# The experts' first loads, statistics and products, moved across the border from attention

## Chip, cores and metric

The kernel runs on one core of one Trainium2 chip. The metric is the device time of one execution in microseconds (us), as the median of several runs. Traces are of one profiled execution.

## What is computed

Input x has 64 batches of 64 rows of 256 numbers. Four residual steps, each on a layer-normalized x: cross attention, a mixture of eight experts beside a shared one (this is where the change lies), a gated pooling attention, a second feed-forward network.

```python
def _L0_ffn_ref(hidden_states, gate_w, w_gate_up, w_down, shared_gate_up, shared_down):
    x = hidden_states.reshape(-1, 256)
    shared_out = _silu_and_mul(x @ shared_gate_up) @ shared_down
    probs = softmax(x @ gate_w, axis=-1)
    topk_w, topk_i = lax.top_k(probs, 2)
    topk_w = topk_w / jnp.sum(topk_w, axis=-1, keepdims=True)
    combine = jnp.sum(one_hot(topk_i, 8) * topk_w[..., None], axis=1)
    ...
    return moe_out + shared_out

x = x + tanh(g_xattn[0]) * _L0_xattn_ref(_layernorm(x), ctx_2048, ...)
x = x + tanh(g_ffn[0]) * _L0_ffn_ref(_layernorm(x), ...)
x = x + tanh(g_xattn[1]) * _L1_xattn_ref(_layernorm(x), ctx_2048, ...)
x = x + tanh(g_ffn[1]) * _L1_ffn_ref(_layernorm(x), ...)
```

## The kernel before

All 4096 rows of x stay in on-chip memory as 32 tiles of 128 rows. Three functions run one after the other, each a block of its own with one instruction stream per engine: `attention`, `experts`, `gate_and_ffn`. The streams meet at semaphores alone, and each engine takes its instructions in the order in which they are written, so that order sets the order of the work. Engines are TensorE (PE), VectorE (DVE), ScalarE (ACT), GpSimd (POOL) and SyncE (SP, which here issues transfers).

**Attention** is a pipeline over tiles. `steps` calls `body(n, n, 0)` for some first n, a hardware loop for the middle and then n = 26 to 33. In `body(n)` an engine works on several tiles at once: scores of tile n+1, exponentials and products of tile n, the output of tile n-2. In the last bodies (n = 31, 32, 33) only the late parts are left; this is the drain. DVE's `normalize_out` (L413, L417), PE's turns and the output product (L592, L631, L652), ACT's copies (L480, L484, L488) and POOL's addition into x (L341) form its chain. SP's last instruction is `q_st<-m_rows` of tile 31 (L241), for which PE waits before the score products of tile 31 (`m_stacked`, in `score_step`).

**Experts**, first half: for eight groups of 512 rows (four tiles) the router and the shared expert. For a group j:

- DVE `stats_of(j)`, POOL `rstd_of(j)` (1/sqrt by a power of -0.5, L929 and L932), DVE `shift_of(j)`, ACT `norm_of(j)` (L1048) make normalized rows `xn`.
- PE `turn(j)` (L1482) transposes them into `t_ps`, ACT `high_of(j)` (L1040) and DVE `low_of(j)` (L1155) split the result into a high and a low part: products are made of three matmuls, high by high, low by high, high by low.
- PE `make_wide(j)` (L1491) multiplies by the router's weights, ACT `take_wide(j)` (L1061) copies, PE `make_logits(j)` (L1499) folds, DVE `take_logits(j)` (L1172) reads the logits. DVE `choose(j)` picks two experts a row, ACT `lead_of(j)` (L1055) takes a tanh for the shares, PE `rank(j)` (L1510) counts rows, DVE `slots_of(j)` (from L1225) gives the places, and POOL `send(j)` scatters the rows to memory.
- PE `products(g, m)` (L1522, twelve matmuls, m = 0 to 3, two banks of each result in turn), ACT's silu (L1089), DVE's product (L1406), ACT `high` and DVE `low` (L1398), PE `down(g, m)` (L1534) are the shared expert. PE may fill a bank for m only when the silu and the product of m-2 are done.

Its weights come in three pieces of 512 KB (`stage`, two buffers); `first_high(p)` (ACT, L1066) and `first_low(p)` (DVE, L1162) split them. The second half runs the eight experts over sorted tiles.

PE's order at the start, before:

```python
turn(0)
pe.wait_ge(s["router_split"], 1)
make_wide(0)
make_logits(0)
turn(1)
make_wide(1)
...
for g in range(GROUPS):
    if g == 0:
        pe.wait_ge(s["first_split"], 2)
    for m in range(CHUNKS):
        products(g, m)
```

## Time and profile before

| what | value |
|---|---|
| median of 3 runs | 1432.47 us (1432.46 to 1432.76) |
| the profiled execution | 1434.49 us, span 1432.8 us |
| PE, DVE, ACT, POOL busy | 93%, 65%, 53%, 48% of the span |
| mean granted clock of PE | 0.969 of full speed |

From the page, in 40 slices of 35.8 us each (tenths of busy time; PEclk: tenths of the full clock):

```profile
PE   4899999999999589998998999999987999999998
DVE  7799999999997278766554333333335766665553
ACT  0477777777778544432342333333426656665642
POOL 7577777777772156443675223310044554445210
PEclk9999999999999789999999999999976999999999
```

The fourteenth slice, from 466 to 501 us, is the border between attention and the experts. A "busy" engine is executing, an idle one waits at a semaphore or has nothing; timelines give behind each instruction the idle time ahead of it and what ended it. The span is from the first to the last instruction, and the profiled execution's own time is 1.7 us more than its span.

### The profile page before, as it was taken

What the parts mean: (1) busy time and instruction counts of PE and PEld (TensorE: products, weight loads), DVE (VectorE), ACT (ScalarE), POOL (GpSimd) and SP (SyncE); (2) the same over time, 40 slices, a digit from 0 to 9 for tenths busy, and PEclk for the clock granted to TensorE, in tenths of its full rate; (3) what the DMA queues carried; (4) which work ended last, traced back from release to release, by engine and by line L of the source; (5) the groups of instructions that cost most, each with busy time, mean ns of one, the idle gap of its engine ahead of it and who ended that gap; (6) DMA issues with size and microseconds to landing.
All of it is one profiled execution on the core that took longest, in us unless ns stands there. A gap on an engine that the chain in (4) does not pass through costs nothing. (4 is left out here: it accounts for less than half of the span.)

```text
span 1432.8 us, 31669 instructions
## 1 busy us (share of the span) xinstructions
PE 1334.9 (93%) x9954; PEld 1017.8 (71%) x9955; DVE 925.9 (65%) x1689; ACT 756.2 (53%) x1461; POOL 686.2 (48%) x853
## 2 busy tenths in 40 slices
PE   4899999999999589998998999999987999999998
PEld 3555555555555268887877888888876788888887
DVE  7799999999997278766554333333335766665553
ACT  0477777777778544432342333333426656665642
POOL 7577777777772156443675223310044554445210
PEclk9999999999999789999999999999976999999999
DMA  3222222222221122114732333241131110111000
GB/s 103 79 81 83 79 88 82 73 86 85 78 73 38 51 83 80 60 59 138 238 124 82 97 97 95 67 142 51 45 96 41 30 44 28 34 45 30 15 16 30
DMA packets 85891, 105.53 MB, mean 74 GB/s; under 512 B 11249, under 2 KB 76145, under 8 KB 85425
## 3 DMA queue, kind: packets, MB, share of 16 engines
q1 hardware_dynamic: 75344, 70.38, 15.5%
q0 software_dynamic: 10464, 34.09, 7.5%
q8 instruction: 47, 0.77, 0.2%
q14 instruction: 36, 0.29, 0.1%
HBM read 53.05 MB, written 23.99 MB: 54 GB/s over the span
## 5 line engine op out<-in xcount | busy, mean ns | idle before, releaser
L469 ACT ACTIVATE e_t<-st_ps 128x512 f32<-128x512 f32 x512 | 278.5, 597 | 105.5 <-PE st_ps L557 101.9
L407 DVE TENSOR_REDUCE row_max<-s_ps 128x4 f32<-128x1024 f32 x256 | 311.3, 1218 | 21.8 <-PE s_ps L562 19.5
L584 PE MATMUL o_ps<-e_t,v_st 128*32 128x256 f32 x2048 | 166.5, 398 | 0.1
L557 PE MATMUL st_ps<-q_st,k_st 32*128 32x256 f32 x1024 | 160.5, 333 | 6.2 <-DMA q_st<-m_rows 3.6
L562 PE MATMUL s_ps<-k_st,q_st 32*128 32x256 f32 x1024 | 158.1, 342 | 5.1 <-DVE row_max L407 3.5
L557 PEld LDWEIGHTS st_ps<-q_st,k_st 32*128 32x128 f32 x1024 | 106.1, 187 | 56.0 <-issue 36.3
L1773 POOL DMA_INDIRECT gathered_tail<-sorted_results,result_at x64 | 70.8, 1106 | 125.3 <-POOLq L2299 107.2
L1640 PE MATMUL y_ps_moe<-w_all_moe,xt_hi_moe 128*128 x568 | 116.5, 286 | 7.7 <-DVE xt_lo_moe L1440 7.7
L2039 DVE TENSOR_TENSOR h_all_tail<-silu_tail,u_ps_tail 128x512 f32<-128x512 f32 x64 | 43.8, 685 | 118.7 <-ACT silu_tail L1888 64.5
L1446 DVE TENSOR_TENSOR h_all_moe<-silu_moe,u_ps_moe 128x512 f32<-128x512 f32 x71 | 48.8, 687 | 109.3 <-PE u_ps_moe L1609 109.3
L1124 ACT COPY y_sb_moe<-y_ps_moe 128x256 f32<-128x256 f32 x71 | 26.5, 373 | 162.2 <-PE y_ps_moe L1640 162.2
L562 PEld LDWEIGHTS s_ps<-k_st,q_st 32*128 32x128 f32 x1024 | 104.3, 193 | 7.1 <-DVE row_max L407 4.6
L1609 PE MATMUL g_ps_moe<-w_all_moe,xt_hi_moe 128*128 x284 | 107.3, 418 | 0.0
L1640 PEld LDWEIGHTS y_ps_moe<-w_all_moe,xt_hi_moe 128*128 128x128 f32 x568 | 93.4, 190 | 12.3 <-issue 9.5
L1609 PE MATMUL u_ps_moe<-w_all_moe,xt_hi_moe 128*128 x284 | 101.0, 396 | 0.0
L952 POOL DMA_INDIRECT sorted_rows<-xn_moe,slots_moe x64 | 64.6, 1009 | 51.8 <-DVE slots_moe L1235 34.5
L1436 DVE TENSOR_TENSOR xt_lo_moe<-t_ps_moe,xt_hi_moe 128x256 fp32r<-128x256 f32 x71 | 30.1, 424 | 91.2 <-ACT xt_hi_moe L1106 91.2
L1888 ACT ACTIVATE silu_tail<-g_ps_tail 128x512 f32<-128x512 f32 x64 | 38.0, 594 | 85.3 <-PE g_ps_tail L2209 85.1
L1640 PE MATMUL y_ps_moe<-w_all_moe,xt_lo_moe 128*128 x284 | 80.7, 284 | 0.0
L2221 PE MATMUL y_ps_tail<-w_hi,h_hi_tail 128*128 128x256 f32 x256 | 74.5, 291 | 0.5 <-DVE h_lo_tail L2046 0.5
L1114 ACT ACTIVATE silu_moe<-g_ps_moe 128x512 f32<-128x512 f32 x71 | 42.5, 599 | 58.9 <-PE g_ps_moe L1609 58.9
L2221 PE MATMUL y_ps_tail<-w_lo,h_hi_tail 128*128 128x256 f32 x256 | 72.8, 284 | 0.0
(341 smaller groups left out, 3613.7 us busy)
## 6 DMA issues: line engine op xcount, KB each, us to landing
k_st<-k_part SPq DMA_DIRECT2D x96, 128.0 KB, 2.1
q_st<-q_part SPq DMA_DIRECT2D x96, 128.0 KB
stage_moe<-in_experts POOLq DMA_DIRECT2D x21, 512.0 KB, 4.2
rows_in_moe<-sorted_rows SPq DMA_DIRECT2D x71, 128.0 KB, 2.0
sorted_results<-y_sb_moe SPq DMA_DIRECT2D x71, 128.0 KB, 1.7
c_in<-in_ctx SPq DMA_DIRECT2D x32, 128.0 KB, 2.2
x_sb<-in_x SPq DMA_DIRECT2D x32, 128.0 KB, 2.1
xn_moe<-in_ctx SPq DMA_DIRECT2D x8, 512.0 KB, 4.4
```

The lines of the kernel that those rows point to most:

```text
L407: nc.vector.tensor_reduce(out, s_ps[p % 2][:], AX_X, ALU.max).then_inc(s["max_taken"], 1)
L469: nc.scalar.activation(e_t[t % 4][:, b, :, :], st_ps[:, b, :, :], ACT.Exp, scale=float(DH) ** -0.5)\
L557: last = nc.tensor.matmul(out, w, moving, start=True, stop=True)
L562: last = nc.tensor.matmul(out, w, moving, start=True, stop=True)
L584: last = nc.tensor.matmul(o_ps[32 * j:32 * j + 32, :], values[:, at:at + 32], e_t[(2 * u + j // 2) % 4][:, j % 2, half_, :], start=(half_ ...
L952: pool.indirect_dma_start(out=xs[:, :], out_offset=bass.IndirectOffsetOnAxis(ap=slots[:, w, GT * j + t:GT * j + t + 1], axis=0), in_=xn[j ...
L1446: nc.vector.tensor_tensor(h_all[c % 2][:], silu[c % 2][:], u_ps[c % 2][:], ALU.mult)\
L1609: last = nc.tensor.matmul(bank[c % 2][:], t[b][:, kc * P:(kc + 1) * P], w_flat[:, bass.ds(where + ((w * 3 + kc) * PIECE + base), FF)], sta ...
L1640: last = nc.tensor.matmul(y_ps[:, 2 * ((c - 1) % 2), :], h[:, m * P:(m + 1) * P], w_flat[:, bass.ds(where + ((w * 3 + 2) * PIECE + m * D), ...
L1773: pool.indirect_dma_start(out=gathered[r][:], out_offset=None, in_=ys[:, :], in_offset=bass.IndirectOffsetOnAxis(ap=result_at[:, q // GT, ...
L2039: nc.vector.tensor_tensor(h_all[m % 2][:], silu[m % 2][:], u_ps[n % 2][:], ALU.mult)\
L2221: last = nc.tensor.matmul(y_ps[:, t, :], h[:, m, t * P:(t + 1) * P], w[:, m * D:(m + 1) * D], start=(m == 0 and b == 0 and t % 2 == 0), st ...
```

## The change

- Five small constants and the first two pieces of the shared expert's weights are issued on SP's queue at the end of attention's stream, behind its last transfer, instead of at the start of the experts' block. For that their tiles (names with `_first`) and semaphores are allocated ahead of both blocks, above the place that the experts' first tiles take, and `first_ones` keeps that place in the experts' memory map.
- The statistics of group 0 are made in attention's drain: `first_stats` on DVE in body 31, `first_root` on POOL in body 32, `first_shift` on DVE in body 32. The experts' block has no `stats_of(0)`, `rstd_of(0)`, `shift_of(0)` any more.
- ACT's order is norm_of(0), first_high(0), first_high(1), high_of(0) instead of first_high(0), norm_of(0), high_of(0), first_high(1). DVE has stats_of(1) before first_low(0) as before, but shift_of(1) now stands before low_of(0).
- PE's order is as in the diff: products(0, 0) before make_logits(0), products(0, 1) behind turn(1); the loop leaves these two out.

```diff
+FIRST = (("consts", (P, ROUTE_CONSTS)), ("tri", (P, P)), ("batch_mask", (P, 2)), ("fold", (2 * EXPERTS, EXPERTS)),
+         ("router_w", (P, 2, EXPERTS)), ("stage0", (P, 2 * FF)), ("stage1", (P, 2 * FF)), ("stats", (P, GT, 6)),
+         ("mean_var", (P, GT, 2)), ("var_eps", (P, GT)), ("rstd", (P, GT)), ("shift", (P, GT)), ("half", (P, GT)))
...
@@ attention, sync
             steps(sp, body)
+            for name, src in (("router_w", "router"), ("consts", "route_consts"), ("tri", "tri"),
+                              ("batch_mask", "batch_mask"), ("fold", "fold")):
+                sp.dma_start(first[name][:], dram[src]).then_inc(first_sems["consts_in"], 16)
+            for p in range(2):
+                sp.dma_start(first[f"stage{p}"][:], dram["experts"][0, p]).then_inc(first_sems[f"piece_in{p}"], 16)
@@ attention, gpsimd
+            def first_root():
+
+                nc.gpsimd.memset(first["half"][:], -0.5).then_inc(first_sems["half_set"], 1)
+                pool.wait_ge(first_sems["stats_done"], 1)
+                nc.gpsimd.tensor_scalar(first["var_eps"][:].unsqueeze(2), first["mean_var"][:, :, 1:2], EPS, None, ALU.add)\
+                    .then_inc(first_sems["eps_added"], 1)
...
+                nc.gpsimd.tensor_tensor(first["rstd"][:], first["var_eps"][:], first["half"][:], ALU.pow)\
+                    .then_inc(first_sems["rstd_ready"], 1)
             def body(n, c, i):
+                if isinstance(n, int) and n == TILES:
+                    first_root()
@@ attention, vector
+            def first_stats():
+
+                dve.wait_ge(s["y_free"], 1 + GT)
+                for t in range(GT):
+                    last = nc.vector.bn_stats(first["stats"][:, t, :], x[:, t, :])
...
+            def first_shift():
+                dve.wait_ge(first_sems["rstd_ready"], 1)
...
                 for p in range(STEPS):
+                    if p == 2 and isinstance(n, int) and n == TILES - 1:
+                        first_stats()
+                    if p == 7 and isinstance(n, int) and n == TILES:
+                        first_shift()
@@ experts, sync
-            for dst, src in ((router_w[:], dram["router"]), (consts[:], dram["route_consts"]), (tri[:], dram["tri"]),
-                             (batch_mask[:], dram["batch_mask"]), (fold[:], dram["fold"])):
-                sp.dma_start(dst, src).then_inc(consts_in, 16)
-            for p in range(3):
-                if p == 2:
-                    sp.wait_ge(s["first_split"], 1)
-                sp.dma_start(stage[p % 2][:], dram["experts"][0, p]).then_inc(piece_in[p % 2], 16)
+            sp.wait_ge(s["first_split"], 1)
+            sp.dma_start(stage[0][:], dram["experts"][0, 2]).then_inc(piece_in[0], 16)
@@ experts, gpsimd
-            for j in range(3):
+            for j in (1, 2):
                 rstd_of(j)
@@ experts, scalar
+            norm_of(0)
             first_high(0)
-            norm_of(0)
+            first_high(1)
             high_of(0)
-            first_high(1)
             norm_of(1)
@@ experts, vector
-            stats_of(0)
...
-            shift_of(0)
             stats_of(1)
             first_low(0)
+            shift_of(1)
             low_of(0)
-            shift_of(1)
             first_low(1)
@@ experts, tensor
             make_wide(0)
+            pe.wait_ge(s["first_split"], 2)
+            products(0, 0)
             make_logits(0)
             turn(1)
+            products(0, 1)
             make_wide(1)
...
             for g in range(GROUPS):
-                if g == 0:
-                    pe.wait_ge(s["first_split"], 2)
                 for m in range(CHUNKS):
-                    products(g, m)
+                    if g > 0 or m > 1:
+                        products(g, m)
```

PE's stream from the wide product of group 0 on, before (`t_ps` takes the router's results, `g_ps` the gate's, `xt_hi0` is group 0's high part, `fold` the fold's matrix):

```order
L1491 MATMUL t_ps0_moe<-xt_hi0_moe,router_both_moe 16x512 x2
L1491 MATMUL t_ps0_moe<-xt_lo0_moe,router_high_moe 16x512 x2
L1499 MATMUL t_ps0_moe<-fold_moe,past_moe 128x8 x4
L1482 MATMUL t_ps0_moe<-ident,xn_moe 128x128 x4
L1482 MATMUL t_ps1_moe<-ident,xn_moe 128x128 x4
L1491 MATMUL t_ps0_moe<-xt_hi1_moe,router_both_moe 16x512 x2
L1491 MATMUL t_ps0_moe<-xt_lo1_moe,router_high_moe 16x512 x2
L1522 MATMUL g_ps0_moe<-xt_hi0_moe,w_all_moe 128x512 x2
L1522 MATMUL g_ps0_moe<-xt_lo0_moe,w_all_moe 128x512
```

The same place with the change:

```order
L1523 MATMUL t_ps0_moe<-xt_hi0_moe,router_both_moe 16x512 x2
L1523 MATMUL t_ps0_moe<-xt_lo0_moe,router_high_moe 16x512 x2
L1554 MATMUL g_ps0_moe<-xt_hi0_moe,w_all_moe 128x512 x2
L1554 MATMUL g_ps0_moe<-xt_lo0_moe,w_all_moe 128x512
L1554 MATMUL g_ps0_moe<-xt_hi0_moe,w_all_moe 128x512 x2
L1554 MATMUL g_ps0_moe<-xt_lo0_moe,w_all_moe 128x512
...
L1531 MATMUL t_ps0_moe<-fold_first,past_moe 128x8 x4
L1514 MATMUL t_ps0_moe<-ident,xn_moe 128x128 x4
L1514 MATMUL t_ps1_moe<-ident,xn_moe 128x128 x4
L1554 MATMUL g_ps1_moe<-xt_hi0_moe,w_all_moe 128x512 x2
```

The first product of group 0 (eight rows, twelve matmuls) moved from behind group 1's wide product to a place ahead of group 0's fold, and the second (from `g_ps1`) from behind the rank product to a place behind group 1's turn. In front of the rank product and behind it PE now has no products but the third.

ACT's stream at the start of the experts' block, before (`stage` holds pieces of weights, `past` the wide product):

```order
L1066 CAST w_all_moe<-stage0_moe 128x1024
L1048 ACTIVATE xn_moe<-x_sb,shift_moe,rstd_moe 128x256 x4
L1040 CAST xt_hi0_moe<-t_ps0_moe 128x512
L1040 CAST xt_hi0_moe<-t_ps1_moe 128x512
L1066 CAST w_all_moe<-stage1_moe 128x1024
L1048 ACTIVATE xn_moe<-x_sb,shift_moe,rstd_moe 128x256 x4
L1061 COPY past_moe<-t_ps0_moe 16x512
L1066 CAST w_all_moe<-stage0_moe 128x1024
L1040 CAST xt_hi1_moe<-t_ps0_moe 128x512
L1040 CAST xt_hi1_moe<-t_ps1_moe 128x512
```

With the change:

```order
L1082 ACTIVATE xn_moe<-x_sb,shift_first,rstd_first 128x256 x4
L1100 CAST w_all_moe<-stage0_first 128x1024
L1100 CAST w_all_moe<-stage1_first 128x1024
L1074 CAST xt_hi0_moe<-t_ps0_moe 128x512
L1074 CAST xt_hi0_moe<-t_ps1_moe 128x512
L1082 ACTIVATE xn_moe<-x_sb,shift_first,rstd_first 128x256 x4
L1095 COPY past_moe<-t_ps0_moe 16x512
L1100 CAST w_all_moe<-stage0_first 128x1024
L1074 CAST xt_hi1_moe<-t_ps0_moe 128x512
L1074 CAST xt_hi1_moe<-t_ps1_moe 128x512
```

The normalization of group 0 now comes first, and both casts of weights stand between it and the reading of the turned rows.

## Rows read from the trace of the kernel before

**Rows 1.** Table of stretches (us, busy by engine (instructions), PEclk, DMA share, GB/s).

```profile
485.00:510.00 25.00, 7.85 (x30) 5.47 (x30) 12.22 (x40) 10.36 (x17) 6.24 (x10) 0.53 0.25 75
...
531.00:651.00 120.00, 120.00 (x712) 103.23 (x711) 88.89 (x264) 46.74 (x90) 65.29 (x63) 1.00 0.19 67
```

**Rows 2.** Timelines by engine, 488 to 506 us (start, us, instruction, idle before).

```profile
488.18 0.34 SPq L863 DMA_DIRECT2D router_w_moe<-in_router  x1
...
490.45 8.17 SPq L867 DMA_DIRECT2D stage_moe<-in_experts  x3
...
491.50 0.17 DVE L1372 COPY taken_moe<-consts_moe 128x8 f32<-128x8 f32 x1 [3.16 <-DMA fold_moe<-in_fold]
...
494.10 1.04 POOL L932 TENSOR_TENSOR rstd_moe<-var_eps_moe,half_moe 128x4 f32<-128x4 f32 x1
...
494.20 1.04 ACT L1066 CAST w_all_moe<-stage_moe 128x1024 fp32r<-128x1024 f32 x1 [8.57 <-DMA stage_moe<-in_experts]
...
495.38 2.08 ACT L1048 ACTIVATE xn_moe<-x_sb,shift_moe,rstd_moe 128x256 f32<-128x256 f32 x4
...
497.50 1.97 PE L1482 MATMUL t_ps_moe<-ident,xn_moe 128*128 128x128 f32 x8 [12.48 <-ACT xn_moe L1048]
...
498.66 0.59 ACT L1040 CAST xt_hi_moe<-t_ps_moe 128x512 fp32r<-128x512 f32 x1 [1.21 <-PE t_ps_moe L1482]
...
499.51 0.59 ACT L1040 CAST xt_hi_moe<-t_ps_moe 128x512 fp32r<-128x512 f32 x1 [0.27 <-PE t_ps_moe L1482]
...
500.97 1.01 PE L1491 MATMUL t_ps_moe<-xt_hi_moe,router_both_moe 128*16 128x512 f32 x2 [1.49 <-DVE xt_lo_moe L1155]
...
503.53 1.87 PE L1499 MATMUL t_ps_moe<-fold_moe,past_moe 16*128 16x8 f32 x8 [0.70 <-ACT past_moe L1061]
...
505.44 0.19 DVE L1172 COPY logits_moe<-t_ps_moe 128x32 f32<-128x32 f32 x1 [3.14 <-PE t_ps_moe L1499]
```

**Rows 3.** Timelines from the first logits to the first down product.

```profile
514.80 0.60 ACT L1089 ACTIVATE silu_moe<-g_ps_moe 128x512 f32<-128x512 f32 x1
...
515.66 0.69 DVE L1406 TENSOR_TENSOR h_all_moe<-silu_moe,u_ps_moe 128x512 f32<-128x512 f32 x1 [2.36 <-PE u_ps_moe L1522]
...
517.11 0.19 DVE L1225 TENSOR_TENSOR row_all_moe<-t_ps_moe,chosen_moe 128x32 f32<-128x32 f32 x1 [0.69 <-PE t_ps_moe L1511]
...
522.97 0.69 DVE L1406 TENSOR_TENSOR h_all_moe<-silu_moe,u_ps_moe 128x512 f32<-128x512 f32 x1
...
524.40 0.47 PE L1534 MATMUL y_ps_moe<-w_all_moe,h_hi_moe 128*128 128x256 f32 x2 [0.76 <-DVE h_lo_moe L1398]
```

**Rows 4.** Timelines of attention's drain.

```profile
463.50 0.62 SPq L241 DMA_DIRECT2D q_st<-m_rows  x1
...
467.48 0.69 PE L557 MATMUL st_ps<-q_st,k_st 32*128 32x256 f32 x4
...
467.59 0.26 DVE L413 RECIPROCAL o_rcp<-misc 128x16 f32<-128x16 f32 x1 [5.24 <-PE misc L592]
...
482.34 0.72 POOL L341 TENSOR_TENSOR x_sb<-x_sb,y_sb 128x256 f32<-128x256 f32 x1 [10.02 <-ACT y_sb L488]
```

**Rows 5.** PE's timeline, the first shared products of group 0.

```profile
509.82 1.03 PE L1491 MATMUL t_ps_moe<-xt_hi_moe,router_both_moe 128*16 128x512 f32 x2 [2.10 <-DVE xt_lo_moe L1155]
...
511.51 1.05 PE L1522 MATMUL g_ps_moe<-xt_hi_moe,w_all_moe 128*128 128x512 f32 x2
...
515.46 1.05 PE L1499 MATMUL t_ps_moe<-fold_moe,past_moe 16*128 16x8 f32 x8
...
516.91 0.71 PE L1522 MATMUL g_ps_moe<-xt_hi_moe,w_all_moe 128*128 128x512 f32 x2
...
519.79 0.64 PE L1522 MATMUL g_ps_moe<-xt_hi_moe,w_all_moe 128*128 128x512 f32 x2
```

**Rows 6.** PE's timeline, the last group's down products.

```profile
670.70 0.69 PE L1534 MATMUL y_ps_moe<-w_all_moe,h_hi_moe 128*128 128x256 f32 x2 [1.99 <-DVE h_lo_moe L1398]
```

**Rows 7.** Table of stretches, PE alone, behind that gap.

```profile
670.80:674.20 3.40, 3.40 (x17) 0.51 0.91 289
```

More of the change, by code:

```diff
@@ L1 @@
 import itertools
+import math
 from contextlib import ExitStack
@@ L66, in wait_alone, with attention @@
     eng.nop(nofuse=True)
-def attention(nc, dram, x, ident, tanh_gain):
+def attention(nc, dram, x, ident, tanh_gain, first, first_sems):
     HP = 2 * HEADS
@@ L421, in normalize_out @@
                     ALU.mult).then_inc(s["o_normed"], 1)
+            def first_stats():
+                dve.wait_ge(s["y_free"], 1 + GT)
+                for t in range(GT):
+                    last = nc.vector.bn_stats(first["stats"][:, t, :], x[:, t, :])
+                last.then_inc(first_sems["stats_raw"], 1)
+                dve.wait_ge(first_sems["stats_raw"], 1)
+                for t in range(GT):
+                    last = nc.vector.bn_aggr(first["mean_var"][:, t, :], first["stats"][:, t, :])
+                last.then_inc(first_sems["stats_done"], 1)
+            def first_shift():
+                dve.wait_ge(first_sems["rstd_ready"], 1)
+                nc.vector.scalar_tensor_tensor(out=first["shift"][:].unsqueeze(2), in0=first["mean_var"][:, :, 0:1], scalar=-1.0,
+                                               in1=first["rstd"][:].unsqueeze(2), op0=ALU.mult, op1=ALU.mult)\
+                    .then_inc(first_sems["shifted"], 1)
             def body(n, c, i):
                 for p in range(STEPS):
+                    if p == 2 and isinstance(n, int) and n == TILES - 1:
+                        first_stats()
+                    if p == 7 and isinstance(n, int) and n == TILES:
+                        first_shift()
                     if p == 0 and there(n, c, 0):
@@ L708, in experts @@
         w_all = sb("w_all", [P, 3, 2, 3, PIECE], F32R)
-        consts = sb("consts", [P, ROUTE_CONSTS])
+        sb("first_ones", [P, FIRST_FLOATS])
+        consts, tri, batch_mask, fold, router_w = (first[name] for name in "consts tri batch_mask fold router_w".split())
+        stage = [first["stage0"], first["stage1"]]
+        stats, mean_var, var_eps, rstd, shift, half = \
+            (first[name] for name in "stats mean_var var_eps rstd shift half".split())
         def const(name):
@@ L719, in experts @@
         w_flat = w_all[:].rearrange("p r s c n -> p (r s c n)")
-        stage = [sb(f"stage{r}", [P, PIECE]) for r in range(2)]
-        router_w = sb("router_w", [P, 2, ROUTER])
         router_both = sb("router_both", [P, 2, 2, ROUTER], F32R)
         router_high = sb("router_high", [P, 2, 2, ROUTER], F32R)
-        fold = sb("fold", [2 * ROUTER, ROUTER])
-        stats = sb("stats", [P, GT, 6])
-        mean_var = sb("mean_var", [P, GT, 2])
-        var_eps = sb("var_eps", [P, GT])
-        rstd = sb("rstd", [P, GT])
-        shift = sb("shift", [P, GT])
-        half = sb("half", [P, GT])
         xn = [xn_all[:, r, :, :] for r in range(XN_RING)]
@@ L805, in experts @@
         total_ps = t_ps[1][:, GT * ROUTER:(GT + 1) * ROUTER]
-        consts_in, zeros_set, filled = sem("consts_in"), sem("zeros_set"), sem("filled")
-        piece_in = [sem(f"piece_in{r}") for r in range(2)]
+        consts_in, zeros_set, filled = first_sems["consts_in"], sem("zeros_set"), sem("filled")
+        piece_in = [first_sems[f"piece_in{r}"] for r in range(2)]
         piece_brought = [sem(f"piece_brought{r}") for r in range(2)]
@@ L918, in _ @@
         def _(pool):
-            nc.gpsimd.memset(half[:], -0.5).then_inc(s["half_set"], 1)
             nc.gpsimd.memset(ones[:], 1.0).then_inc(s["ones_set"], 1)
@@ L2282, in program @@
         ys = nc.dram_tensor("sorted_results", (TILES_MAX * P, D), F32, kind="Internal").ap()
+        with ExitStack() as ahead:
+            ahead.enter_context(nc.sbuf_tensor("below_first", [P, EXPERTS_BELOW], F32))
+            first = {name: ahead.enter_context(nc.sbuf_tensor(name + "_first", list(shape), F32)) for name, shape in FIRST}
+        first_sems = {name: nc.alloc_semaphore(name + "_first") for name in
+                      "consts_in piece_in0 piece_in1 half_set stats_raw stats_done eps_added rstd_ready shifted".split()}
         with nc.cleanup_on_exit():
-            attention(nc, dram, x, ident, tanh_gain)
+            attention(nc, dram, x, ident, tanh_gain, first, first_sems)
         with ExitStack() as early:
```

13 lines of the change are left out of this document (8 added, 5 removed).

## The prediction

> **What bounds the kernel now.** I read the page's forty slices first. TensorE (PE) is busy nine tenths nearly everywhere; the first hole behind the start is the slice from 466 to 501 us, with five tenths and a granted clock of seven. So I asked the table of stretches for the border between attention and the experts' phase. From 485 to 510 us PE works 7.85 of 25 us at a mean clock of 0.53; from 531 to 651 us it works 120.00 of 120 us at 1.00 [rows 1]. The second row is what makes the first worth reading: behind the border the phase is bound by PE alone, so each us by which PE gets there sooner comes off the end, until something takes it back.
>
> The timelines give the chain at the border [rows 2]. The experts' block starts at 488.18 on SP's queue. VectorE (DVE) waits for five small loads until 491.50; GpSimd (POOL) makes the root at 494.10; ScalarE (ACT) waits 8.57 us for a piece of weights, casts it at 494.20 and only then normalizes, at 495.38; PE, idle for 12.48 us, turns the rows at 497.50. Then come the wide router product at 500.97 and its fold at 503.53, and DVE has the first logits at 505.44. I call this moment T. From T on the chain is DVE's and ACT's, not PE's [rows 3]: silu at 514.80 (ACT has the routing's tanh and a table load ahead of it), the product at 515.66, the slots at 517.11, then group 1's routing, the next product at 522.97, and PE's first down product at 524.40.
>
> **The change, part by part.**
>
> *What moves into the drain* costs nothing that I can find. The statistics go ahead of DVE's step at 467.59, before which it idles 5.24 us [rows 4]; they need less than the 2.6 us that lie between 491.50 and the root at 494.10 today [rows 2]. They wait for x tiles finished long before. The root (1.04 us and a small addition) goes ahead of POOL's addition at 482.34, before which it idles 10.02 us. The shift is one small DVE instruction in the same idle drain, with its root long made. On SP's queue seven transfers (1.2 MB) go behind the last q_st<-m_rows of 463.50, with nothing of attention behind them. What it costs if that cover fails is rival 3.
>
> *The start.* The block still starts at 488.2. ACT can normalize at once: 2.1 us, to 490.35, where it now ends at 497.46: 7.1 sooner. From there to PE's wide product it is 3.5 us today; 1.5 of them ACT waits for PE's turning (1.21 and 0.27). In its place come two casts of weights, 2 x 1.04 with a little overlap, 2.0 us. So it is 4.0 now, and the wide product comes at 494.3 instead of 500.97 [rows 2]. DVE's low half of weights and statistics of group 1 run beside that, and group 1 is normalized by about 495.4, before PE asks.
>
> *The first products go in front of the fold.* The wide product, four matmuls of 512 columns, takes 1.7 us at half clock (509.82 to 511.51), so they start at 496.0. Twelve of the same width cost 12 x 0.425 = 5.1 us at half clock and 2.9 at the full one (516.91 to 519.79) [rows 5]. When does the clock rise? Today PE worked without a gap from 509.8 and had the full clock 3.9 us later, in bursts from 497.5 on it had not. The same lag behind 494.3 gives 498.2; the late end is not before the fold. I take 500.1, near the late end, since the bursts since 490.4 are short. Then 4.1 us of products run at half clock, the last fifth at the full one (0.6): they end at 500.7. The fold takes 1.0 at full clock (515.46), 1.9 at half (503.53). So T comes at 501.7 instead of 505.44: 3.7 us. Without the products in front it would come some 4 us sooner; this edit pays here, to be repaid later.
>
> *From T to the first down product.* DVE has the same work between T and the routing's end, and the product then waits for silu alone: T + 10.0 where it was T + 10.2. The slots were held until 517.11 by the rank product, behind other PE work; now PE has less in front of it and waits for the routing, so the slots follow the product at once, 0.75 us sooner. Together 0.95: the product of 522.97 comes at 518.3, the down product of 524.40 at 519.75, a gain of 3.7 + 0.95 = 4.65 [rows 3].
>
> *What PE's new idling costs.* Its second products are done before the routing, so it has nothing between the turning of group 2 (ACT has normalized it at about 515.0, PE is through at 516.1) and 519.75: 3.65 us. Behind a gap of 1.99 us that ended at 670.70 [rows 6] the clock stood at 0.51 for the 3.4 us from 670.8, in which PE worked without pause [rows 7]. At half clock 3.4 us do the work of 1.9 (0.24 over 0.425), so such a spell costs 1.5 us, and PE bounds the phase there. I book one; its bounds are nothing, and 2.0 for a spell of 4.4 us that starts before 519.75. A rule of the Trainium skill speaks against this change in the same sense: "TensorE: Matmul & The Clock Gate", section "HAM oscillation — how this bites in real kernels", has bursts with waits between them fall to the half clock again and again, and advises to run the products together. By it the two waits around the rank product, close together, and the one before the down product would bring two spells, one more than I book: 1430.8.
>
> *The rest* (names of tiles, a spacer in the memory map, nine semaphores that live longer) moves no instruction of the steady groups.
>
> **Sum.** -4.65 + 1.5 = -3.15 us. The profiled execution took 1434.49 us with a span of 1432.8, that is 2.0 more than the median of the runs, 1432.47. The stage counts the same in both, so I take it from the median: **1429.3 us**. About 0.2%, 2.9 us, is what a measurement of this kernel can tell from no change, and the forecast lies just beyond it.
>
> **Rivals.**
>
> 1. *No spell is paid.* PE idles before the third products too (two waits from about 508.8 to 511.7, the small rank product between). If the clock falls there, these run at half clock in time that PE has to spare, bring the clock back, and the down product starts at full clock. For it: the waits are as long as the one of rows 6. Against: it hangs on tenths of a us. The 1.5 is not paid: 1427.8.
>
> 2. *The clock comes back later, or falls once more.* If products and fold all run at half clock (5.1 + 1.9), T is 503.0, 1.3 us later: 1430.6. One more spell, that of the waits in rival 1 but still there when the down product starts: 1430.8. For it: PE ran at half clock through all bursts from 497.50 to 511.51. Against: none of them was as long as the one that now begins at 494.3.
>
> 3. *The drain is delayed, and the kernel is slower.* The 1.2 MB are issued from about 464.1, right behind the q_st<-m_rows of 463.50, for which PE's step at 467.48 waits [rows 4]. If the DMA engines mix the two, the small one lands with the large ones. It decides if it lands after 467.5, 4.0 us from its issue. The price: one 512 KB piece took 3.75 us from 490.45 to the cast at 494.20 [rows 2], two take 7.5; from 464.1 that is 471.6, 4.1 us late, and net +1.0: 1433.4, at worst 1436. Against: m_rows stands first in the queue.
>
> 4. *Spells of later phases move.* The page shows the clock low again at the border to the last phase; gaps there and the fall of rows 7 may meet it otherwise once all comes 3 us sooner. Each spell is 1.5 us either way. It has no time of its own; it widens the range.
>
> **How the numbers follow.** Forecast 0.45 (own range 1428.3 to 1430.3: 0.5 for the longer spell, 0.5 for T, 1.0 for a T by the early end); rival 1 0.27; rival 2 0.18; rival 3 0.05; rival 4 with more than one spell 0.05. The range takes rival 1 with one late spell spared, 1426.3, and rival 2 with 0.4 of room, 1431.2. Faster by over 0.2% is under 1429.6: 0.7 of the forecast's share, rival 1, and a little of the others: 0.62. Within 0.2%: the rest of the forecast, rival 2, most of rival 3: 0.35. Slower by over 0.2% is above 1435.3: 0.03.
>
> **What would show it.** ACT's first normalization at 488.3, PE's turning at 490.4, the wide product at 494.3, the first logits at 501.7; the down product at 519.75, behind some 3.6 us of idle time that DVE's h_lo ends; half clock for about 3.4 us behind it, or, for rival 1, a low stretch that is over before 519. Nothing before 488 moves, PE at 467.48 above all. I am wrong if the block starts later than 488.5, if T comes after 503.5, or if the gain at the down product, less the spell, is not there at 651 us too.

## The result and the profile after

The changed kernel takes 1426.1 us (median of 5 runs, 1423.94 to 1428.27), the kernel before 1432.7 us beside it (5 runs, 1432.46 to 1433.94): ratio 0.995, 95% interval 0.9936 to 0.9965. The forecast was 1429.3 us with a range from 1426.3 to 1431.2. So the sign was right, the gain, 6.6 us, is twice the 3.15 foreseen, and the time lies 0.2 us below the range. All runs of the two unchanged kernels together give means of 1432.63 (112 runs, standard error 0.2) and 1426.58 (45 runs, 0.3), a difference of 6.05 with a standard error of 0.35 us; one execution of the kernel before, of 3834.5 us, is left out. The runs of one kernel are spread over 7 to 9 us, which the three runs seen at first (within 0.3 us) did not tell.

The profiled execution of the changed kernel took 1428.27 us, with a span of 1426.6. Its table of stretches, for the windows of [rows 1] (the first one, and the second moved 5 us up with the work):

```profile
485.00:510.00 25.00, 16.87 (x70) 12.33 (x71) 14.38 (x47) 12.71 (x22) 3.82 (x6) 0.70 0.21 64
526.00:646.00 120.00, 120.00 (x713) 103.41 (x712) 86.83 (x264) 46.70 (x90) 61.74 (x61) 1.00 0.19 66
```

PE works 16.87 us where it worked 7.85, and behind the border it is still the only bound. The border itself, by engine (start, us, instruction, idle before), in the order of [rows 2], from SP's last m_rows on:

```profile
461.21 0.62 SPq L248 DMA_DIRECT2D q_st<-m_rows  x1
...
464.25 0.90 SPq L279 DMA_DIRECT2D stage_first<-in_experts  x2
...
470.41 1.04 POOL L344 TENSOR_TENSOR rstd_first<-var_eps_first,half_first 128x4 f32<-128x4 f32 x1
...
478.08 0.15 DVE L461 SCALAR_TENSOR_TENSOR shift_first<-mean_var_first,rstd_first 128x4 f32<-128x4 f32 x1
...
483.40 0.72 POOL L366 TENSOR_TENSOR x_sb<-x_sb,y_sb 128x256 f32<-128x256 f32 x1 [2.65 <-ACT y_sb L534]
...
485.76 2.07 ACT L1082 ACTIVATE xn_moe<-x_sb,shift_first,rstd_first 128x256 f32<-128x256 f32 x4 [2.44 <-PEq L2325]
...
487.89 1.97 PE L1514 MATMUL t_ps_moe<-ident,xn_moe 128*128 128x128 f32 x8 [5.17 <-ACT xn_moe L1082]
...
491.67 1.01 PE L1523 MATMUL t_ps_moe<-xt_hi_moe,router_both_moe 128*16 128x512 f32 x2 [1.81 <-DVE xt_lo_moe L1189]
...
493.33 1.06 PE L1554 MATMUL g_ps_moe<-xt_hi_moe,w_all_moe 128*128 128x512 f32 x2
...
498.09 1.05 PE L1531 MATMUL t_ps_moe<-fold_first,past_moe 16*128 16x8 f32 x8
...
499.18 0.19 DVE L1206 COPY logits_moe<-t_ps_moe 128x32 f32<-128x32 f32 x1 [6.53 <-PE t_ps_moe L1531]
```

Now ACT normalizes 2.4 us behind attention's last addition into x (POOL, 483.40); before, it waited for the weights at this place. The first products stand between the wide product and the fold, whose 1.05 us is the time at full clock. The same chain as [rows 3] and [rows 5], from these first logits, T, to the first down product:

```profile
507.11 0.41 PE L1542 MATMUL t_ps_moe<-chosen_moe,tri_first 128*128 128x32 f32 x2 [0.67 <-DVE taken_moe L1250]
...
509.19 1.22 PE L1554 MATMUL g_ps_moe<-xt_hi_moe,w_all_moe 128*128 128x512 f32 x2 [1.46 <-ACT silu_moe L1123]
...
509.23 0.69 DVE L1438 TENSOR_TENSOR h_all_moe<-silu_moe,u_ps_moe 128x512 f32<-128x512 f32 x1 [2.18 <-issue]
...
509.91 0.18 DVE L1259 TENSOR_TENSOR row_all_moe<-t_ps_moe,chosen_moe 128x32 f32<-128x32 f32 x1
...
516.09 0.69 DVE L1438 TENSOR_TENSOR h_all_moe<-silu_moe,u_ps_moe 128x512 f32<-128x512 f32 x1
...
517.52 0.47 PE L1566 MATMUL y_ps_moe<-w_all_moe,h_hi_moe 128*128 128x256 f32 x2 [1.99 <-DVE h_lo_moe L1430]
```

And PE's stretches around that gap, and where [rows 6, 7] had the other one (PE busy, granted clock, DMA share, GB/s):

```profile
507.60:514.50 6.90, 5.44 (x15) 0.51 0.10 36
...
517.90:521.30 3.40, 3.40 (x15) 0.50 0.33 116
```

```profile
665.35 0.50 PE L1566 MATMUL y_ps_moe<-w_all_moe,h_hi_moe 128*128 128x256 f32 x2 [2.00 <-DVE h_lo_moe L1430]
```

```profile
665.40:668.80 3.40, 3.30 (x26) 1.00 0.96 284
```

These are PE's first matmul behind that gap, and the stretch that follows. The clock is low over the third products, which have time to spare, and again for 3.4 us behind the first down product, where PE bounds the phase. The fall behind the last group's gap of 2 us did not come: 1.00 where [rows 7] have 0.51.

One more thing stands in these rows. Attention's last addition into x starts at 483.40, where it was at 485.71:

```profile
485.71 0.72 POOL L341 TENSOR_TENSOR x_sb<-x_sb,y_sb 128x256 f32<-128x256 f32 x1 [2.65 <-ACT y_sb L488]
```

So 2.3 us of the difference between the two traces lie in attention. I therefore measure from that addition, so that what happened in attention drops out. The theory to be tested, A: attention's end moves by chance. The rival, B: the change itself shortens attention.

### The profile page after: what moved, and what is told of

It is laid out like the page before. It is cut to its first block and busy times, and to the rows that moved or that the text cites. A ratio compares the mean times of both kernels' runs of the same rounds, so it can differ in the third digit from the quotient of the medians.

```text
span 1426.6 us, 31668 instructions
## 1 busy us (share of the span) xinstructions
PE 1331.1 (93%) x9954; PEld 1015.6 (71%) x9955; DVE 924.2 (65%) x1689; ACT 757.5 (53%) x1461; POOL 683.9 (48%) x853
## 5 line engine op out<-in xcount | busy, mean ns | idle before, releaser
L1674 PE MATMUL y_ps_moe<-w_all_moe,xt_hi_moe 128*128 x568 | 113.1, 284 | 8.1 <-DVE xt_lo_moe L1472 8.1
L1158 ACT COPY y_sb_moe<-y_ps_moe 128x256 f32<-128x256 f32 x71 | 26.4, 372 | 157.6 <-PE y_ps_moe L1674 157.6
L2255 PE MATMUL y_ps_tail<-w_hi,h_lo_tail 128*128 128x256 f32 x256 | 73.0, 285 | 0.0
```

The lines of the kernel that those rows point to most:

```text
L1674: last = nc.tensor.matmul(y_ps[:, 2 * ((c - 1) % 2), :], h[:, m * P:(m + 1) * P], w_flat[:, bass.ds(where + ((w * 3 + 2) * PIECE + m * D), ...
L2255: last = nc.tensor.matmul(y_ps[:, t, :], h[:, m, t * P:(t + 1) * P], w[:, m * D:(m + 1) * D], start=(m == 0 and b == 0 and t % 2 == 0), st ...
```

## The experiments

The table gives, from the trace of each run, the start of the last addition into x, the distance from it to T, to the first down product (D) and to the end of the span, and the mean of the timed runs. The column "D to G" is the distance from the first down product to G, PE's first down product of the last group ([rows 6], 670.70 in the kernel before); PE bounds that stretch. "Burst" is explained at e5. The experiments ran on four chips, on which the means of the kernel before are 1432.3 to 1432.9 us.

| kernel (run) | last addition | T | D | D to G | end | mean us (runs) |
|---|---|---|---|---|---|---|
| before | 485.71 | 19.73 | 38.69 | 146.3 | 947.1 | 1432.63 (112) |
| before, again (e1) | 481.03 | 19.88 | 38.39 | 146.3 | 946.1 | |
| before, again (e16) | 483.58 | 19.74 | 39.14 | 146.3 | 948.0 | |
| changed | 483.40 | 15.78 | 34.12 | 147.8 | 943.2 | 1426.58 (45) |
| changed, again (e2) | 486.05 | 15.50 | 33.84 | 147.8 | 942.6 | |
| changed, again (e13) | 480.84 | 15.47 | 33.82 | 147.8 | 942.7 | |
| changed, again (e14) | 483.35 | 15.72 | 34.06 | 147.8 | 942.5 | |
| changed, again (e15) | 482.21 | 15.26 | 33.61 | 147.7 | 942.7 | |
| drain part alone (e3) | 483.32 | 12.46 | 32.56 | 146.3 | 941.4 | 1425.51 (6) |
| order part alone (e4) | 486.36 | 22.38 | 40.38 | 146.3 | 948.9 | 1434.81 (12) |
| before + burst (e5) | 480.11 | 19.76 | 38.86 | 146.3 | 947.7 | 1429.82 (12) |
| changed + burst (e6) | 481.99 | 15.20 | 33.55 | 147.7 | 942.2 | 1424.84 (8, with e10 to e12) |
| changed + burst (e10) | 479.56 | 14.75 | 33.08 | 146.3 | 940.9 | |
| changed + burst (e11) | 483.84 | 15.75 | 34.08 | 147.8 | 943.4 | |
| changed + burst (e12) | 484.27 | 15.51 | 33.85 | 147.8 | 943.4 | |
| products behind turn (e7) | 483.17 | 12.45 | 28.69 | 146.3 | 937.6 | 1422.84 (5) |
| the same, kept busy (e8) | 485.05 | 12.48 | 31.62 | 146.3 | 941.6 | 1425.77 (6) |
| e7 + burst (e9) | 482.25 | 12.45 | 30.04 | 146.4 | 938.7 | 1421.35 (6) |

**Both kernels unchanged (e1, e2).**

> The kernel before, unchanged, once more, to learn what single executions differ by. Theory A (chance): attention's end moves between executions of one kernel by about 2 us, with the moment at which the clock first rises (63.3 us in the trace of before, 57.0 in that of the changed kernel); then this trace may show the last addition into x anywhere from 483.4 to 485.7. Theory B (cause): the changed kernel's attention is faster because of the change; then it is at 485.7 +- 0.2 again. Time within 1 us of 1432.7 by either.

> The changed kernel, unchanged, once more. Theory A: the last addition into x lies anywhere from 483.4 to 485.7; Theory B: at 483.4 +- 0.2. From there to the first down product it is 34.1 us in both theories (38.7 in the kernel before). Time: 1424 to 1428.5.

The kernel before took 1433.41 us (12 runs, ratio 1.0009, 0.9997 to 1.002), the changed one 1426.23 (7 runs, 0.996, 0.9943 to 0.9976). In the new traces the last addition comes at 481.03 in the kernel before and at 486.05 in the changed one: the order of the first pair is turned round. Both lie outside the 483.4 to 485.7 that I had given theory A, so the chance is larger than I had thought. What stays is the distance to T and to the down product. So single traces can't be compared by their ends: attention's end moves by up to 5 us. Where? The first addition into x tells; these are POOL's, of the kernel before, and of e1:

```profile
82.65 0.73 POOL L341 TENSOR_TENSOR x_sb<-x_sb,y_sb 128x256 f32 x1
```

```profile
78.35 0.73 POOL L341 TENSOR_TENSOR x_sb<-x_sb,y_sb 128x256 f32 x1
```

The 4.3 us are there before the first tile is done. From its fifth to its 29th addition attention takes 321.8 to 322.1 us in all 18 traces. What differs at the start is when PE's clock first rises: the 256-column matmuls of the scores fall from 0.41 to 0.28 us at 64.3 us in the kernel before, at 51.2 in e1, at 57.3 in the changed kernel and at 66.4 in e2. The earlier this rise, the earlier the first addition into x, by about a third of a microsecond each, and with the change no otherwise than without it: 78.35 in e1 (rise at 51) beside 78.07 in e13, where the clock is full from 50.5 on.

**One part of the change alone (e3, e4).** e3 is the changed kernel with the order of the kernel before on PE, ACT and DVE; e4 is the kernel before with this edit and its counterparts on ACT and DVE:

```diff
             make_wide(0)
+            pe.wait_ge(s["first_split"], 2)
+            products(0, 0)
             make_logits(0)
             turn(1)
+            products(0, 1)
             make_wide(1)
```

> The changed kernel with the order of PE, ScalarE and VectorE around the first products as it was before; loads and statistics of group 0 stay in attention's drain. Theory 1 (both parts of the change gain): slower than the changed kernel by 1 to 3 us. Theory 2 (the drain part gains all, the products in front give part of it back): the logits of group 0 come 13.2 us behind attention's last addition (15.8 in the changed kernel, 19.7 before), all of the 7.0 us arrives at the first down product, and no spell at half clock stands behind it: 1425.7 against before's 1432.7, that is 2 to 3.5 us faster than the changed kernel where both have the same clock in attention.

> The kernel before with nothing in the drain, but with the changed order of PE, ScalarE and VectorE around the first products. Theory 1: faster than before by 1 to 3 us. Theory 2: the logits of group 0 come 4.2 us later than in the kernel before, 0.95 comes back at the slots, and PE pays a spell of 1.3 to 1.5 us behind its wait for the first down product: slower than before by 3 to 5 us, 1436 to 1438.

The drain part alone took 1425.93 us (6 runs, 0.9949, 0.9931 to 0.9967), the order alone 1434.88 (12 runs, 1.0011, 1.0 to 1.0022). By the table, the drain part brings T 7.3 us nearer to attention's end. The order takes 3.1 of them back (15.55 against 12.46), repays 1.75 behind T (18.35 against 20.10 to the down product), and costs another 1.5 between D and G, where the changed kernel has its half-clock spell and e3 has none. Behind G it gets 1.4 back, and what remains is the 1.3 us between the ends (942.7 against 941.4). In e4 the order costs 2.6 in T and repays 0.95, but here no spell stands behind the down product. So the drain part makes the whole gain, and the order that goes with it is a small loss. The timed runs say the same with less certainty: e4's mean is 2.2 us (standard error 0.6) above the kernel before, and e3's 1.1 us below the changed kernel, which is hardly more than its standard error of 0.8. Theory 2 had both larger: 3 to 5 us for e4, with T 4.2 us later, and 2 to 3.5 us for e3. Of e3, what holds its down product back:

```profile
495.78 0.19 DVE L1206 COPY logits_moe<-t_ps_moe 128x32 f32<-128x32 f32 x1 [3.18 <-PE t_ps_moe L1531]
...
500.16 1.03 PE L1523 MATMUL t_ps_moe<-xt_hi_moe,router_both_moe 128*16 128x512 f32 x2 [2.10 <-DVE xt_lo_moe L1189]
...
506.80 0.69 DVE L1438 TENSOR_TENSOR h_all_moe<-silu_moe,u_ps_moe 128x512 f32<-128x512 f32 x1 [3.15 <-PE u_ps_moe L1554]
...
515.88 0.47 PE L1566 MATMUL y_ps_moe<-w_all_moe,h_hi_moe 128*128 128x256 f32 x2 [1.11 <-DVE h_lo_moe L1430]
```

DVE waits 3.15 us for products that PE began only behind the second wide product, in front of which PE itself waited 2.10 us. That hole is where the products belong (e7).

**The clock's first rise, made early (e5, e6).** In the wait of 3.57 us for m_rows near 40 us:

```diff
                 for p in range(STEPS):
+                    if isinstance(n, int) and n == 0 and p == LAG:
+                        keep_busy(20)
                     score_step(n, c, i, p)
```

where keep_busy writes matmuls of 128x256 into score PSUM that is not yet in use.

> The kernel before, with 20 matmuls of 128x256 whose result nobody reads, put into TensorE's wait for m_rows in front of the first turned scores (38.9 to 42.4 us in the traces). Nothing else differs, and they cost nothing where the wait hides them. Theory A (the 2.3 us by which attention ended earlier in the profiled changed kernel is chance: the moment of the clock's first rise, 51 to 66 us in the six traces so far, moves the last addition into x by some 0.3 us for each microsecond): the rise comes at or before 46 us in each run, attention's end moves to 480 to 482 us, the median falls by 3 to 5 us to about 1428.5, and the spread of the runs, 8.3 us for the kernel before, shrinks to below 4 us. Theory B (the change itself makes attention shorter, by its placement of memory or its earlier loads): the median of this kernel still stands 5.5 to 6.5 us above that of the same edit in the changed kernel. If the burst is too short to raise the clock, time and spread are those of the kernel before (1432.9).

> The changed kernel with the same 20 matmuls in the same wait. Theory A: attention ends in its trace within 0.5 us of where it ends with the burst in the kernel before, and the difference of the two medians is what the traces show between the last addition into x and the end of the span, 3.7 us (3.0 to 4.4). Theory B: the difference stays 5.5 to 6.5 us, and attention ends some 2 us earlier here than there.

e5 took 1429.47 us (12 runs, 0.9982, 0.9969 to 0.9994), e6 1423.01 (5 runs, 0.9933, 0.9914 to 0.9951). The burst (these 20 matmuls) is worth 2.8 us by the means in the kernel before: the start's half clock is real time. In the changed kernel it is worth 2.9 by e6's five runs, and 1.7 with the three later executions (e10 to e12). The spread of e5 did not fall below 4 us; it was 4.95. The difference of the two medians, 6.5 us, spoke for B (with the three later executions the means are 5.0 apart), but their traces did not: in the trace of e6 attention ended later, not sooner, than in e5, because the clock had fallen in attention's drain:

```profile
470.80:477.60 6.80, 6.80 (x44) 0.50 0.00 0
```

The drain, from the 29th to the last addition, took 29.1 us there (452.88 to 481.99) and 26.4 to 26.9 in 15 other traces; e4 and e9 are the two others with 29.1. These 2.7 us are a second piece of chance.

**The products in the hole behind group 1's turn (e7).** From e3:

```diff
             turn(1)
+            pe.wait_ge(s["first_split"], 2)
+            products(0, 0)
             make_wide(1)
             pe.wait_ge(s["ones_set"], 1)
+            rank(0)
             for g in range(GROUPS):
```

with ACT's first silu behind high_of(1), and group 1's copy of the wide logits behind lead_of(0).

> The part in attention's drain alone, but with the first products behind group 1's turn (in its wait of 2.1 us for xt_lo) and in front of its wide logits, ScalarE's first silu in front of the copy of the wide logits, and the rank matmuls in front of the fold. Theory (the block's start is a chain through VectorE; products in front of the logits of group 0 lengthen it, products in the wait behind them don't): logits of group 0 stay 12.5 us behind the last addition into x, as with the drain part alone (changed kernel 15.8); the first h_all comes 8 to 8.5 us behind the logits (11.0 with the drain part alone), the slots start by about 10 us (12.5), and the first down product comes 17.5 to 18.5 us behind the logits (20.1), so 30 to 31 us behind the last addition (32.6; changed kernel 34.1; before 38.6). Median 1.5 to 2.5 us below the drain part alone, about 1424. Rival: TensorE is what counts, its wait is only moved, and the median is that of the drain part alone (1425.9 +- 0.8).

It took 1422.75 us (5 runs, 0.9931, 0.9913 to 0.995), 10.9 below the kernel before in that comparison and 3.7 below the changed kernel by the means. Its rows:

```profile
495.62 0.19 DVE L1209 COPY logits_moe<-t_ps_moe 128x32 f32<-128x32 f32 x1 [3.18 <-PE t_ps_moe L1534]
...
497.55 1.20 PE L1557 MATMUL g_ps_moe<-xt_hi_moe,w_all_moe 128*128 128x512 f32 x2
...
503.52 0.69 DVE L1441 TENSOR_TENSOR h_all_moe<-silu_moe,u_ps_moe 128x512 f32<-128x512 f32 x1
...
511.86 0.47 PE L1569 MATMUL y_ps_moe<-w_all_moe,h_hi_moe 128*128 128x256 f32 x2
```

T is as early as in e3, h_all comes 7.9 us behind it instead of 11.0, and the down product 16.2, better than the 17.5 expected: PE has no wait of note in front of it, and in this trace the clock stood at full from 501.4 to 658.4 us. The rival, that the wait is only moved, is refuted: from the last addition to the end it is 937.6 us against e3's 941.4, and the mean is 2.7 us (standard error 0.8) below e3's.

**PE kept busy over its waits (e8).** e7 with matmuls whose results nobody reads in PE's waits from attention's last steps to the first fold. The experts' part of the edit:

```diff
+            keep_busy(4)
             turn(0)
             pe.wait_ge(s["router_split"], 1)
+            keep_busy(4)
             make_wide(0)
+            keep_busy(1)
             make_logits(0)
```

In attention 5, 5 and 5 of them go into the last body and 22 behind it.

> The same, with TensorE's waits from attention's last three steps to the fold of group 0 filled with matmuls whose results nobody reads (5, 5, 5 and 22 of 128x256 in attention's last waits, then 4, 4 and 1 of f32 128x256), so that its clock has no reason to fall. Theory (at the border TensorE lies on the chain at half clock: turn 1.97, wide logits 2.1, fold 1.87, turn 1.94 us, products 5.1): the granted clock stays 1.00 from 475 us to the down products, the turn takes about 1.0, the fold about 1.0, the logits come 9.5 to 10.5 us behind the last addition (12.5), and the median falls by another 2 to 4 us, to 1420 to 1422. Rival: the clock falls all the same, the filling matmuls then take twice their time and delay the turn and the wide logits, and the kernel is 2 to 4 us slower than without them.

1425.9 us (6 runs, 0.9948, 0.9928 to 0.9968), 3 us slower than e7. The time is the one that the rival gave, but what led to it is in neither of the two. The clock did stay at full until 506.5, and the turn took 1.09 us; yet T came 12.48 us behind attention's end, as before:

```profile
488.27 1.96 PE L1587 MATMUL g_ps_moe<-x_sb,ident 128*128 128x256 f32 x8 [1.28 <-PEq L2343]
...
490.38 1.09 PE L1526 MATMUL t_ps_moe<-ident,xn_moe 128*128 128x128 f32 x8
...
496.44 1.05 PE L1543 MATMUL t_ps_moe<-fold_first,past_moe 16*128 16x8 f32 x8 [1.11 <-ACT past_moe L1104]
...
505.50 0.38 PE L1554 MATMUL t_ps_moe<-chosen_moe,tri_first 128*128 128x32 f32 x2 [2.49 <-issue]
```

```profile
493.84 2.08 ACT L1091 ACTIVATE xn_moe<-x_sb,shift_first,rstd_first 128x256 f32<-128x256 f32 x4 [0.68 <-DVE shift_first L1194]
```

The 22 matmuls at attention's end held the blocks' common border back (the experts' block begins 3.2 us behind the last addition, 2.4 in e7), and a PE that is ready sooner meets ACT, whose 2.08 us for group 1 stand in front of the copy that the fold needs. And in the next wait, 2.49 us for the routing, the clock fell after all, from 506.5 to 513.4, over products that are late in this order. Here, holding the clock cost more than it gave.

**e7 with the burst (e9), and three more executions of e6's kernel (e10 to e12).**

> The version with the first products behind group 1's turn (1422.8) with the 20 matmuls in attention's wait for m_rows (which gave 2.9 us in the kernel before and 2.7 in the changed one, by the means). If the two add up: 1419 to 1420.5, 13 to 14 us below the kernel before, last addition into x at 479.5 to 482 us, logits 12.5 and the first down product 28.7 us behind it. Rival: the version's own luck with the clock (its five runs lie within 1.3 us) is part of its time, and with the burst it comes out no lower than 1422.

> The changed kernel with the burst once more, for its trace alone. The three traces of the changed order so far all hold a half-clock spell over the third products (two periods of 3.4 us) and one over the first down products, mean clock .971, .971 and .968; other runs of it reach .973. Theory C (the spells of the block's start are chance too: whether the pause of 1.5 to 2 us in front of the third products or the first down product brings a fall depends on the phase of the clock's decisions): among three more traces at least one has no half-clock spell between 505 and 525 us or only the first one, its mean clock is .972 or .973 and its time 1422.3 to 1423.0, 1.5 to 3 us below the traced 1425.9 of before. Theory D (the spells are fixed): all three show them, and the low times come from somewhere else.

> As for the look before it: the same kernel, another execution.

> As for the first of these looks: the same kernel, a third execution.

e9 took 1421.14 us (6 runs, 0.9918, 0.9897 to 0.9939): the best version, 11.1 below the kernel before. The burst gave 1.5 us here by the means, not 2.9, and with 6 runs over 5.8 us that is barely told apart from nothing; its own trace has the fall in the drain. I had expected 13 to 14 us below and the down product at 28.7; it came at 30.04, behind a half-clock spell from 505.2 to 508.6 that e7 does not have. The single executions of e10 to e12 took 1422.22, 1428.86 and 1429.36 us. e10 is the execution without a spell behind the down product that theory C asked for:

```profile
512.64 0.48 PE L1574 MATMUL y_ps_moe<-w_all_moe,h_hi_moe 128*128 128x256 f32 x2 [2.54 <-DVE h_lo_moe L1438]
```

```profile
512.60:516.00 3.40, 3.36 (x20) 1.00 0.32 113
```

A wait of 2.54 us, longer than the 1.99 of the changed kernel's trace, and the clock stays at full behind it. Of the nine traces of the changed kernel, with and without the burst, it has the shortest way from attention's end to the span's, 940.9 us. And it gives the price of the spell. These are G in e10, and G in e1, with the stretch behind it:

```profile
658.95 0.50 PE L1574 MATMUL y_ps_moe<-w_all_moe,h_hi_moe 128*128 128x256 f32 x2 [2.00 <-DVE h_lo_moe L1438]
```

```profile
665.72 0.50 PE L1534 MATMUL y_ps_moe<-w_all_moe,h_hi_moe 128*128 128x256 f32 x2 [1.98 <-DVE h_lo_moe L1398]
```

```profile
665.60:669.00 3.40, 3.28 (x26) 1.00 0.78 245
```

From D to G it is 658.95 - 512.64 = 146.31 us, as in all ten traces without a spell behind the down product (146.3 to 146.4); in the eight traces with it, it is 147.7 to 147.8 (665.35 - 517.52 = 147.83). So the spell costs 1.5 us. The last group's fall [rows 7] stands in eight of the ten traces without the first spell, and in none of the eight with it; the two without either are e1 and e10. In e4 a wait of 2.04 us in front of the down product brought no fall either:

```profile
526.74 0.48 PE L1534 MATMUL y_ps_moe<-w_all_moe,h_hi_moe 128*128 128x256 f32 x2 [2.04 <-DVE h_lo_moe L1398]
```

```profile
526.70:530.10 3.40, 3.36 (x20) 1.00 0.22 77
```

e11 and e12 show why the burst is no cure: in both the clock rose by the burst, fell again at 47 us, and came back at 57, and attention ended as late as without it (first addition of e11 at 80.90, of e6 at 76.65).

**More runs (e13 to e16).**

> The changed kernel unchanged, to tell how much of its gain lies outside the stretches that the traces explain. So far its twelve runs mean 1426.7 against 1432.8 for 69 runs of the kernel before: 6.1 +- 0.7. From the last addition into x to the end of the span the six traces of the changed order stand on average 4.3 us below the three of the order before (4.2 to 6.7 with the clock). Theory A (the remaining 1.8 is chance of a small sample): with 15 to 30 runs more the mean settles at 1427.5 to 1428.8, 4 to 5.3 us below the kernel before. Theory B (attention itself ends earlier in the changed kernel): the mean stays at 1426.2 to 1427.2, and the last additions into x in the new traces lie around 482 us, 2 us below those of the kernel before.

> As for the run before: the same kernel, more executions and one more trace.

> As for the two before: the same kernel, more executions and one more trace.

> The kernel before once more, on the same chip as the three runs of the changed one: a mean of 1432.3 to 1433.3, and a trace whose distance from the last addition into x to the end of the span is 946 to 948 us, as in the three so far (946.1, 947.1, 947.7).

The changed kernel took 1425.65 (9 runs, 0.9967, 0.9953 to 0.9981), 1425.55 (12 runs, 0.9958, 0.9946 to 0.9971) and 1426.52 us (12 runs, 0.9966, 0.9953 to 0.9978), the kernel before 1433.19 (12 runs, 1.0003, 0.999 to 1.0016). The mean of the 33 runs, 1426.54, is where theory B had put it, and A was wrong there. The last additions of the three new traces lie at 482.1 on average, also as B said. But over all unchanged traces they are 483.2 with the change (five) and 483.4 without (three). The middle of attention and its drain take the same time with and without the change, and the first additions stand at 82.65, 78.35 and 80.56 in the kernel before and at 80.79, 83.31, 78.07, 80.35 and 79.49 in the changed one, means of 80.5 and 80.4. With a scatter of 2 us, this finds no sign of B but can't exclude an effect of 1 to 2 us.

What the traces account for is 947.1 - 942.7 = 4.35 us; the timed runs say 6.05, with a standard error of 0.35. The other 1.7 is not placed, but the record says where to look. The eight traced executions are themselves only 4.6 us apart by their own times (means 1432.2 and 1427.6), so most of it lies in executions without a trace. Of the 45 runs of the changed kernel 15 have a mean granted clock of 0.972 or more; they take 1425.2 us on average, the other 30 1427.3, and all five traces are of the second kind (0.970 or 0.971). e10, the execution without the spell, has 0.973. And 13 of 107 runs of the kernel before, but only one of 45 of the changed one, have 0.967 or less, where no trace of either lies; the three traces with the fall in the drain have 0.966 to 0.968. Together these two shares are worth about 1 us (an estimate from the means of these groups). That the runs at 0.972 and more are executions without the spell, and those at 0.967 and less executions with the fall in the drain, is likely but not shown.

## Why the forecast was wrong

The forecast was a gain of 3.15 us, and 6.6 came. This is how the 3.45 between them divide:

| stretch | forecast | measured |
|---|---|---|
| last addition to D | -4.65 | -4.85 (38.74 to 33.89) |
| D to G, the spell | +1.5 | +1.5 (146.3 to 147.8) |
| G to the end | 0 | -1.0 (762.0 to 761.0) |
| not placed by any trace | 0 | -1.7 |
| these five runs against the means of all | 0 | -0.55 |

The first three are means over the unchanged kernels' traces, three and five.

**The chain at the border: right, in part by luck.** The block's start did not move against attention; in the trace of the changed kernel the wide product comes 8.27 us behind the last addition (491.67), against 15.26 (500.97 and 485.71): 7.0 sooner, forecast 6.7. T is 3.95 nearer in that pair and 4.2 over all, forecast 3.7. From T to D it is 0.6 less, forecast 0.95. The two errors are of opposite sign, and the sum came out closer than its terms. I had the clock rise at 500.1, near the late end; against the last addition it came about 0.4 us sooner, and made the fold a full-clock one as forecast.

**The drain: right.** The statistics, root, shift and loads lie in idle time; attention's drain takes 26.4 us with them and 26.4 to 26.8 without. Rival 3 found nothing to stand on.

**The first products: right in sign.** "This edit pays here, to be repaid later": measured against the drain part alone, it pays 3.1 us (I had said 4) and is repaid 1.75 up to the down product, and then it has the spell to pay.

**The spell: right in size, and partly for another reason.** The gap was 1.99 us long, not 3.65, since the third products ran at half clock and PE came late to it; so rival 1's condition was met, but not its outcome: the low stretch ended at 514.5, and a new one began at 517.9 all the same. Rival 1 came true in one of nine traces, e10. The price that I had booked, 1.5 us, is the measured one. The 1430.8 that I had worked out by the Trainium skill ("TensorE: Matmul & The Clock Gate", section "HAM oscillation — how this bites in real kernels") did not come. Two low stretches did stand there, but the one of the waits around the rank product, 507.6 to 514.5, lay where PE has time to spare. The section's own case also has longer waits between its bursts than these two, so the second spell was my reading of it and not what it states.

**The step that failed** is rival 4: "Each spell is 1.5 us either way. It has no time of its own." The half clock behind the last group's gap [rows 7] is in two of the three unchanged traces of the kernel before (and in e5, not in e1), and in none of the nine of the changed kernel. That is a term of its own: 1.5 us times two in three is 1.0, and from G to the end the changed kernel gains 762.0 - 761.0 = 1.0 us (e1, which has no such fall, takes 761.3 there, the two with it 762.1 and 762.6). With it the forecast would have been 1428.3. Other spells come and go too (3.4 us at 730.2 in e1, at 712.7 in e13, at 729.4 in e14), and no cost of theirs shows in G to the end. I had seen the row and used it for its price only, without asking whether it would still be there.

**The second failure** is the range. "Nothing before 488 moves" is true of the program and not of the time: the moment of the clock's first rise moves all of it by several us from run to run, a fall in the drain by 2.7. I read three runs within 0.3 us as the spread of the kernel. With a scatter of 2 us for one run, a median of five carries near 1 us of chance, and the range should have been about that much wider on both sides. The largest piece, the 1.7 us, I can give no step for: its cause stays open.

## What to carry to other kernels

Before a trace is compared with another, choose a row that the change can't reach (here the last addition into x) and measure from it; what lies ahead of it can be the luck of one execution. When work is put into a wait, look for the wait whose end is not on the chain: the same products cost 3.1 us in front of the first logits and nothing in the hole behind them. A half-clock spell in a row of the old kernel is a term that the change may remove, just as it may add one. And where the mean clock of the timed runs is on record, see whether the traced ones are like the others before their difference is taken for the kernel's.

## What was not expected of the hardware

- The same program has its clock's first rise at 51 to 66 us, and with it the first addition into x moves by 5 us (78.07 to 83.31); 20 matmuls in a wait bring it forward, but in two of six traces it fell again for 10 us.
- In these traces a wait's length does not tell whether the clock falls: it stayed at 1.00 behind 2.54 us of idle time in e10 and 2.04 us in e4, and was at 0.50 within 0.4 us of the first down product's start in the eight other traces of the changed kernel, with the burst or without, behind waits of 1.99 to 2.32 us.
- A spell of 3.4 us at half clock, where PE is the bound, costs 1.5 us: from D to G it is 147.7 to 147.8 us with it and 146.3 to 146.4 without, over 18 traces.
- In e6 the clock fell at 470.8 us although PE had been busy for 6.27 of the 6.8 us from 464.0 on, with no single wait above 0.3 us; the same matmuls with the same waits went by at full clock in the changed kernel's own trace.
